# GpSimd takes over the splitting of the third slot's routed weights in a fused transformer layer

## The reference, cut to what matters

```python
def _expert(x, w_up, w_down):
    h = gelu(einsum('bsh,hf->bsf', x, w_up), approximate=False)
    return einsum('bsf,fh->bsh', h, w_down)
shared_out = _expert(x, shared_up[0], shared_down[0])
probs = softmax(einsum('bsh,he->bse', x, router_w))
top_k_prob, top_k_idx = top_k(probs, 2)
gates = one_hot(top_k_idx) weighted by top_k_prob
for e in range(8):
    routed_out += gates[..., e:e+1] * _expert(x, routed_up[e], routed_down[e])
return shared_out + routed_out + x
```

## Time and profile before

| what | us |
|---|---|
| median of the runs | 337.52 |
| the profiled execution, its own time | 339.28 |
| its span, first to last instruction | 337.4 |
| TensorE busy | 302.1 |
| GpSimd busy | 206.2 |
| VectorE busy | 162.0 |
| ScalarE busy | 147.7 |
| mean granted TensorE clock | 0.98 |

### The profile page before, as it was taken

One profiled execution on the slowest core, in us unless ns is written; L12 is line 12 of the kernel. 1 busy time (PEld: TensorE's weight loads), 2 busy tenths in 40 slices (PEclk: granted clock), 3 DMA queues, 4 the chain that ended last, 5 costly groups with the idle time before them and its releaser, 6 DMA issues.

```text
span 337.4 us, 6656 instructions
## 1 busy us (share of the span) xinstructions
PE 302.1 (90%) x2049; PEld 270.4 (80%) x2050; DVE 162.0 (48%) x404; ACT 147.7 (44%) x331; POOL 206.2 (61%) x164
## 2 busy tenths in 40 slices
PE   0896988989998789999899999999999999999970
PEld 0474878977787789998699989998999899899960
DVE  3598596988835397463224332332333233324220
ACT  2786133277978252642443334333433443344210
POOL 3275172438790001666988898898888899335551
PEclk9997899999999998999999999999999999999997
DMA  7994004014355230475443265255343533224532
GB/s 243 308 229 160 18 26 155 2 48 147 88 189 170 88 101 2 124 235 206 165 166 114 111 202 171 46 171 187 119 124 92 170 56 47 47 30 47 64 33 29
DMA packets 21924, 39.90 MB, mean 118 GB/s; under 512 B 2913, under 2 KB 18226, under 8 KB 19602
## 3 DMA queue, kind: packets, MB, share of 16 engines
q0 software_dynamic: 7456, 25.43, 27.9%
q1 hardware_dynamic: 14162, 14.03, 13.5%
q10 hardware_dynamic: 288, 0.20, 0.3%
HBM read 28.84 MB, written 6.93 MB: 106 GB/s over the span
## 4 chain that ended last, share of the span: by engine, by line
PE 43%; POOL 13%; DMA 11%; issue 10%; DVE 9%; ACT 3%; POOLq 3%; SPq 0%; DVEq 0%; ACTq 0%
DMA out_tokens<-xy_all,dest 10%; PE ps L986 9%; PE ps L987 8%; PE ps L988 8%; PE ps L1036 7%; POOL ring L444 6%; PE ps L858 4%; POOL ring L443 3%; POOL out_tokens L587 3%; PE ps L886 2%; POOLq L584 2%; PE ps L956 2%; PE ps L1108 1%; DVE h L1300 1%; DVE ps L1272 1%
## 5 line engine op out<-in xcount | busy, mean ns | idle before, releaser
L444 POOL TENSOR_TENSOR ring<-stage,ring 128x512 fp32r<-128x512 f32 (+2 forms) x30 | 76.2, 2541 | 2.5
L1566 DVE TENSOR_TENSOR hgT<-ps,hgT 128x512 fp32r<-128x512 f32 x50 | 32.2, 687 | 72.3 <-ACT hgT L848 72.3
L986 PE MATMUL ps<-ring,hgT 128*128 x200 | 58.0, 290 | 2.1 <-DVE xy_all L1572 1.5
L587 POOL DMA_INDIRECT out_tokens<-xy_all,dest x25 | 39.5, 1582 | 27.6 <-DMA out_tokens<-xy_all,dest 15.3
L988 PE MATMUL ps<-ring,hgT 128*128 x200 | 55.9, 279 | 0.0
L987 PE MATMUL ps<-ring,hgT 128*128 x200 | 55.9, 279 | 0.0
L840 ACT ACTIVATE hg<-ps 128x512 f32<-128x512 f32 x50 | 29.9, 599 | 47.7 <-PE ps L988 47.7
L577 POOL DMA_INDIRECT xy_all<-normalized_tokens,dest x25 | 25.1, 1006 | 38.8 <-DVE dest L1528 31.5
L986 PE MATMUL ps<-ring,xgT 128*128 x100 | 41.3, 413 | 1.1 <-issue 0.6
L443 POOL TENSOR_SCALAR ring<-stage 128x512 fp32r<-128x512 f32 (+2 forms) x30 | 38.5, 1284 | 2.7 <-PEq L1122 2.5
L986 PEld LDWEIGHTS ps<-ring,hgT 128*128 128x128 f32 x200 | 37.6, 188 | 2.5 <-issue 2.5
(11 more groups left out here) (194 smaller groups left out, 591.5 us busy)
## 6 DMA issues: line engine op xcount, KB each, us to landing
stage<-in_w_up POOLq DMA_DIRECT2D x9, 1024.0 KB, 5.5
stage<-in_w_dn POOLq DMA_DIRECT2D x9, 1024.0 KB, 5.5
xg<-xy_all SPq DMA_DIRECT2D x25, 128.0 KB, 2.0
xp<-in_patches SPq DMA_DIRECT2D x4, 384.0 KB, 7.9
normalized_tokens<-hn SPq DMA_DIRECT2D x4, 276.0 KB
residual_tokens<-h SPq DMA_DIRECT2D x4, 276.0 KB
ring<-in_tok_w SPq DMA_DIRECT2D x1, 768.0 KB, 6.7
base<-residual_tokens SPq DMA_DIRECT2D x2, 384.0 KB, 3.6
```

The source lines that it names most:

```text
L444: return nc.gpsimd.tensor_tensor(lo, stage[:, part, c0:c1], hi.bitcast(F32), ALU.subtract)
L587: pool.indirect_dma_start(out, bass.IndirectOffsetOnAxis(ap=dest[:, t:t + 1].bitcast(U32), axis=0), xy_all[:, t, :], None, compute_op=ALU. ...
L986: nc.tensor.matmul(o, a[0], b[0], start=n == 0, stop=False)
L1566: v.tensor_tensor(hgT[:, c, 1, 4 * half:4 * half + 4, :], ps[:, turned_bank + half, :].rearrange("p (k t) -> p k t", k=4), hgT[:, c, 0, 4 ...
```

## The change

GpSimd splits x = 2 by its own `piece`, directly behind x = 1 and behind a wait for `base_kept`; each half's `piece` issues its own weight load, and the eighth also `turn_done(2)`. `expert_high`, `expert_low` and `p_high` are gone, and the 13 gathers stand together. VectorE's `shared_end` of the second group now stands behind low part 18, where it stood ahead of it.

```diff
@@ gpsimd
             for n in range(4, 8):
                 piece(1, n)
+            pool.wait_ge(base_kept, 16 * NG)
+            for n in range(8):
+                piece(2, n)
...
-            gather_rows(0, 6)
-            load_weights(6)
-            gather_rows(6, 10)
-            load_weights(7)
-            turn_done(2)
-            gather_rows(10, FREE_ROWS)
+            gather_rows(0, FREE_ROWS)
             prepare_half(3, 0)
@@ scalar
-            def expert_high(n):
-                part, k = n // 4, n % 4
-                if k == 0:
-                    act.wait_ge(w_in[part], 16 * 3)
-                if n == 0:
-                    act.wait_ge(base_kept, 16 * NG)
-                c = slice(UPW * part + 512 * k, UPW * part + 512 * (k + 1))
-                nc.scalar.activation(ring[:, 2, 0, c], stage[:, part, 512 * k:512 * (k + 1)], ACT.Copy).then_inc(p_high, 1)
...
-            shared_act(8, 11)
-            for n in range(8):
-                shared_act(11 + n, 12 + n)
-                expert_high(n)
-            shared_act(19, NSG * KF)
+            shared_act(8, NSG * KF)
@@ vector
-            def expert_low(n):
-                part, k = n // 4, n % 4
-                dve.wait_ge(p_high, n + 1)
-                c = slice(UPW * part + 512 * k, UPW * part + 512 * (k + 1))
-                last = v.tensor_tensor(ring[:, 2, 1, c], stage[:, part, 512 * k:512 * (k + 1)],
-                                       ring[:, 2, 0, c].bitcast(F32), ALU.subtract)
-                if k == 3:
-                    last.then_inc(w_free, 1)
-            shared_parts(TABLE_AT, TABLE_AT + 1)
-            for n in range(8):
-                expert_low(n)
-                if n < 2:
-                    shared_parts(TABLE_AT + 1 + n, TABLE_AT + 2 + n)
-                elif n == 2:
-                    shared_end(SG, 2 * SG)
-                else:
-                    shared_parts(TABLE_AT + n, TABLE_AT + 1 + n)
+            shared_parts(TABLE_AT, 2 * KF + LAG)
+            shared_end(SG, 2 * SG)
+            shared_parts(2 * KF + LAG, 3 * KF - 1)
```

More of the change, by code:

```diff
@@ L235, in fusion_layer @@
         rows_in = [sem(f"rows_in{i}") for i in range(4)]
-        p_high = sem("p_high")
         slot_free = sem("slot_free")
```

## The result

The changed kernel takes **344.82 us** (median of 4 runs, 344.03 to 346.31) against 337.47 us (4 runs, 337.37 to 338.18): ratio 1.0213 [1.0187, 1.0239], 7.35 us slower. The direction, the place and the mechanism are the predicted ones and the time lies inside the range, but the forecast was 3.35 us. The sum had less than half of the loss.

The account below looks back on a forecast made before the run. TensorE was taken as the bound, waiting for VectorE's routing ahead of the table; 3.0 us (VectorE held up) + 0.35 (moved sum) = 3.35 us on the median of 337.52 gave 340.9 us, range 337.8 to 345.0.

Parts of the forecast that it names:

- the 10.4 us of pieces: Eight ScalarE copies and eight VectorE subtractions removed beside TensorE's shared steps: worth 0, since TensorE waits for neither.
- The moved sum: Second group's `shared_end` behind low part 18: TensorE's 0.23 us wait for `base` grows by 0.35 us, on the path.
- GpSimd would not become the bound: Gathers end at 160.2, shared steps at 160.9 us: hidden with 0.7 us; the opposite case, 341.2, had chance 0.08.
- the last cover: Low part 15, behind `dest`: done about 140.0, wanted by up product 17 at 141.25 us; hidden with 1.2 us.
- the clock: TensorE mostly at 1.2 GHz from 132.6 to 136.1 us: change put at 0, range minus 1.2 to plus 1.6.
- the term that decides: VectorE's routing instructions, 120.27 to 128.30 us, wait for GpSimd's instruction under way: table 3.0 us late.
- the walk: Step through 11 VectorE instructions between 120.27 and 128.30 us, order of arrival deciding, waits added up: 3.0 us.
- The bound that the prediction itself worked out for that case: Same VectorE stretch ahead of the table, if groups of unlinked instructions are broken up too: 4.3 us.
- the 5.5 us that the prediction gives: Same VectorE stretch by the Trainium skill's rule, every wait full length: about 5.5 us in place of 3.0.
- rival a: Heavier wait before the table, or another clock fall: 6 or 4.3 + 1.6, and 0.35; 343.8 to 344; chance 0.16.
- the signs named: L1478, L1487, L1495 up to 1.5 us; TensorE's wait near 123.6 some 2; `base` 0.6; `dest` 139.5; gather after 142.

Follow-up runs that it names:

- kernel 7: The changed kernel with 26 extra matmuls into an unused bank ahead of up products 11, 13 and 14: 354.5 us, ratio 1.0454.
- kernel 2: The changed kernel with sixteen GpSimd pieces of 256 columns in place of eight of 512: 343.23 us, ratio 1.0159.
- kernel 4: The changed kernel with the second group's `shared_end` put back ahead of low part 18: 344.66 us, ratio 1.0185.
- kernel 8: As kernel 7, but with gathers 7 to 13 behind the first half of x = 3: 353.3 us, ratio 1.0499.
- kernel 1: The kernel before, plus the sixteen GpSimd piece instructions into an idle buffer, nothing taken from ScalarE or VectorE: 345.92 us, ratio 1.0184.
- kernel 9: The kernel before with 9, 2 and 4 extra matmuls ahead of products 11, 12 and 13: 338.17 us, ratio 1.0009.
- kernel 3: The kernel before with sixteen write-only GpSimd fills of 1024 columns in the wait for the table: 340.88 us, ratio 1.0081.
- kernel 5: The kernel before, its pieces kept, with only the second group's sum moved behind low part 18: 339.49 us, ratio 1.0035.
- kernel 6: The changed kernel with GpSimd's pieces held back by one more wait, for `r_told`: 351.02 us, ratio 1.0346.

## Why the prediction was right and wrong

**Right.** That the 10.4 us of pieces were worth nothing against the kernel before: from product 11 to the first routed matmul the three added costs sum to 6.25 us and the traces differ by 6.16, which leaves 0.09 us for anything that removing them gave. The moved sum: 0.30 measured, 0.35 forecast. That GpSimd would not become the bound: it waits 5.71 us at the end of the shared steps. The forecast said 0.7. Of the 5.0 us between, 1.6 is that the shared steps end later, 3.4 that the gathers end earlier: the pieces ended at 139.19, not at 142.3, of which 1.1 us is their earlier start in this profile and 2.0 that they took less time, most likely since GpSimd won turns that I gave to VectorE. Low part 15, the last cover, was done at 140.85, and product 17 wanted it at 142.86. That it stayed hidden was luck in part: `dest` was 2.2 us later than forecast, and without the 1.58 us of the clock product 17 would have wanted it at 141.28, with 0.43 us to spare. And the term that decides was the right one: instructions of VectorE in on-chip memory wait for GpSimd's.

**Wrong, the size of that term.** The sum had 3.0 us; it is 4.37 (4.35 added up from the rows). The step that failed is in the walk: "L1490 to L1492 come directly behind each other and pass", and "L1496 passes with it". Instructions that wait for no semaphore between them were taken as one turn. They are not: in between, GpSimd took its turn, and the 18-column instruction L1492 cost 1.08 us more, L1496 also 1.08. The bound that the prediction itself worked out for that case was 4.3. I chose against it, and a row of the trace before spoke for it. The earlier trace rows show VectorE's L1259 from 25.07 to 25.75 us and GpSimd's instruction from 25.36 on, which waits for it. The next row of VectorE was overlooked:

```profile
25.67 0.95 DVE L1217 SCALAR_TENSOR_TENSOR tt<-tt,trs,ring 128x256 f32<-128x256 f32 x1
```

It stands directly behind L1259, the last thing it needed, GpSimd's `trs`, was there at 25.39, and alone it takes 0.48 us. It ends at 26.62, GpSimd's being shown to 26.33: GpSimd, waiting, had the turn between the two.

The smaller steps erred both ways: L1478 and its twin 1.41 forecast, 0.31 measured; the cast and L1484 0.12 and 0.86 + 0.38; L1487 0.43 and 0.28; L1495 1.07 and 0.36. Together they were forecast 0.84 us too high, and the two unlinked steps 2.16 too low. Some of that is chance: GpSimd began 2.73 us behind product 11 instead of the 2.48 assumed, when the first L1478 was through, and in kernel 7 the same instruction lost 0.94 us. That 4.3 fits to 0.1 us is luck in part. Nor does the 5.5 us that the prediction gives for every wait at full length follow from the lock: the five waits of the walk, each until the shown end and so 0.14 us longer, would sum to some 3.7, an estimate from its own rows.

**Wrong, the clock.** Put at 0, between minus 1.2 and plus 1.6. It is +1.58 in the traces, and kernel 7 shows the same 1.56 from the other side. It isn't the chance of one profile: table to product 17 takes 11.48 us in the changed kernel, 11.50 and 11.45 in kernels 2 and 4, and 9.90 before. With TensorE kept busy through the waits the falls became shorter or went (kernels 7 and 8), so the two terms were not independent. But a longer wait doesn't fix the clock's price: kernel 1 had nearly the same delay, 3.96 us, and 9.88 us from the table to product 17, as before. A chance of its own for a heavier wait or one more fall was there (rival a, 343.8 to 344), but 0.16 was little for it. It gave 4.3 + 1.6 + 0.35 = 6.25 us, what the traces sum up to.

**The rest.** 6.54 us behind product 11 in the two profiled executions, 7.35 between the medians. The profiled execution before stood 1.8 us above its median, with a mean granted clock of 0.980, where the 17 runs of it beside kernels 2, 4, 8 and 9 have a median of 0.983, and the four runs after 0.970. An estimate from these: 0.003 of 340 us is 1.0 us, some 0.6 of a 3.4 us fall to half level (0.005 of the mean), that the typical run before had less than the profiled one. That would cover the 0.8 us between the two differences; in which stretch the unprofiled runs differ isn't shown.

**What would show it.** Of the signs named, these came: L1487's successor L1470 at 0.46 us and L1495's at 0.99 against 0.18 and 0.63; a wait above 2 us ahead of the product near 124 (2.59); `base` at 0.53. The table's matmuls at 131.38 look like the 131.3 forecast, but only because this profile runs 1.34 us ahead; against product 11 they are 14.95 us behind where the forecast had 13.5. GpSimd's pieces began at 119.16 for the same reason, not at 120.3. `dest` came at 140.16, 8.57 us later against product 11 and not 6.4, and the first gather at 140.68, before the 142 named, for GpSimd was free by then.

## What to carry to other kernels

Before work is moved to an idle GpSimd, ask what VectorE does in that time: where it runs a chain of small instructions in on-chip memory that something waits for, each can lose up to one whole GpSimd instruction, so the price is the number of meetings times the length of GpSimd's pieces, and unlinked instructions are no protection. If it has to be there, pieces of half the length halve the price (2.17 for 4.37 us), and operations that only write spare VectorE's two-input ones, though not its copies (still 1.64 us here). Work removed from engines that nobody waits for pays nothing towards that.

## What the runs showed of the hardware

- GpSimd gets in between two VectorE instructions that stand directly behind each other: 1.25 us for 18 columns that take 0.17 alone, 1.70 for 450 columns that take 0.62 (the changed kernel), 0.95 for 256 columns that take 0.48 (the kernel before). It holds in the other direction as well: GpSimd's copy of 512 columns took 2.99 us instead of 0.61 beside a 2.55 us instruction.
- Beside a GpSimd that only writes, two-input instructions of VectorE kept their length, one-input copies and scalings took up to 1.01 us for 0.18 (kernel 3).
- The granted clock falls to its half level for 3.4 us or 6.8 us, and where it does changes from run to run in code that is the same up to there: at 30.1 to 36.9 us before and 32.2 to 35.6 after; at 104.5 us in some kernels that differ only behind it. A 3.4 us fall costs some 1.6 us if TensorE is the bound there. A difference of that size between two single profiles says nothing by itself.
- In four kernels ScalarE stood still with its input there, while GpSimd issued its gathers or just behind them: for 0.83 us (kernel 5), four times for 1.1 to 2.7 us (kernel 1), and in stretches idle of up to 7.31 and 9.12 us (kernels 7 and 6). In the changed kernel, whose row of 13 gathers stands within 0.7 us of where kernel 7 has it, it did not. The length of the row alone doesn't explain it: kernels 1 and 5 have six, then four, then three gathers, as the kernel before has, which doesn't show it. Kernel 8 doesn't either, with six. What ScalarE waited for the profile doesn't show; the cause stays open, and no run was made on it alone. It is a risk of the change that its own profiled run did not meet.
